# Two-layer transformer, attention stage: the refinement of the layer norms' reciprocal root moved from the vector engine to GpSimd

## What is computed

```
x = x + _L0_xattn_ref(_layernorm(x), ctx, ctx, ...)
x = x + _L0_ffn_ref(_layernorm(x), ...)
x = x + _L1_xattn_ref(_layernorm(x), ctx, ctx, mask_SxS2, mask_BxS2, ...)
x = x + _L1_ffn_ref(_layernorm(x), ...)

def _layernorm(x, eps=1e-05):
    m = jnp.mean(x, axis=-1, keepdims=True)
    v = jnp.var(x, axis=-1, keepdims=True)
    return (x - m) / jnp.sqrt(v + eps)
```

## Time and profile before

| | us |
|---|---|
| median of 3 runs | 2528.04 (2525.23 to 2528.23) |
| the profiled execution | 2527.97 |
| its span, first to last instruction | 2526.4 |
| mean granted TensorE clock | 0.953 of full speed |
| busy: PE, DVE, ACT, POOL | 2272.7, 1462.2, 861.7, 464.8 |

### The profile page before, as it was taken

How to read it: one execution, slowest core, us unless ns; L and a number is a source line. 1 busy time by engine, 2 the same in 40 slices (tenths; PEclk the granted TensorE clock), 3 DMA queues, 4 the chain that set the end, 5 groups by cost and what they waited for, 6 DMA issues and landing times. The chain is left out here.

```text
span 2526.4 us, 39469 instructions
## 1 busy us (share of the span) xinstructions
PE 2272.7 (90%) x14663; PEld 1960.2 (78%) x14663; DVE 1462.2 (58%) x3129; ACT 861.7 (34%) x1210; POOL 464.8 (18%) x413
## 2 busy tenths in 40 slices
PE   5888888565899976999999599999999999999999
PEld 3677777543788874877877588888888888888888
DVE  5777777475554526767776485545454545454444
ACT  1454544202444422444444342222222222222222
POOL 3122222200666542222221220000000000000000
PEclk8999999775899997999999799999999999999999
DMA  2021211200444330111211310000000000000000
GB/s 71 26 75 50 75 50 59 73 4 23 108 97 94 65 45 23 68 58 56 69 50 43 127 32 26 25 26 26 26 26 26 26 26 26 26 25 26 24 9 11
DMA packets 117497, 114.85 MB, mean 45 GB/s; under 512 B 15440, under 2 KB 114320, under 8 KB 117392
## 3 DMA queue, kind: packets, MB, share of 16 engines
q1 hardware_dynamic: 105104, 96.29, 12.0%
q0 software_dynamic: 12288, 17.05, 4.1%
HBM read 62.72 MB, written 50.59 MB: 45 GB/s over the span
## 5 line engine op out<-in xcount | busy, mean ns | idle before, releaser
L1802 DVE TENSOR_TENSOR zmix_hid<-zmix_act_gate,psum 128x1024 f32<-128x1024 f32 x128 | 156.3, 1221 | 389.8 <-issue 359.3
L143 PE MATMUL psum<-zmix_wd_hi,zmix_hid_hi 128*128 128x256 f32 x1024 | 289.6, 283 | 1.9 <-DVE zmix_acc L1793 1.7
L145 PE MATMUL psum<-zmix_wd_hi,zmix_hid_lo 128*128 128x256 f32 x1024 | 290.1, 283 | 0.0
L144 PE MATMUL psum<-zmix_wd_lo,zmix_hid_hi 128*128 128x256 f32 x1024 | 290.0, 283 | 0.0
L1746 ACT ACTIVATE zmix_act_gate<-psum 128x1024 f32<-128x1024 f32 x128 | 131.8, 1029 | 403.2 <-PE psum L145 403.2
L1754 ACT ACTIVATE zmix_hid_hi<-zmix_hid 128x1024 fp32r<-128x1024 f32 x128 | 135.5, 1059 | 383.8 <-PE psum L145 285.7
L593 PEld LDWEIGHTS psum<-att_v_cur,att_probs 128*128 128x128 f32 x2048 | 247.4, 193 | 9.5 <-ACT att_probs L693 3.6
L593 PE MATMUL psum<-att_v_cur,att_probs 128*128 128x96 f32 x2048 | 247.2, 275 | 2.7 <-ACT att_probs L693 2.7
L1807 DVE TENSOR_TENSOR zmix_hid_lo<-zmix_hid,zmix_hid_hi 128x1024 fp32r<-128x1024 f32 x128 | 158.7, 1240 | 135.1 <-ACT zmix_hid_hi L1754 134.2
L143 PE MATMUL psum<-zmix_xT_hi,zmix_wg_hi 128*128 128x512 f32 x512 | 203.3, 397 | 12.0 <-DVE zmix_xT_lo L1782 12.0
L1793 DVE SCALAR_TENSOR_TENSOR zmix_acc<-psum,zmix_weight,zmix_acc 128x256 f32<-128x256 f32 x512 | 211.8, 476 | 1.6 <-PE psum L145 1.6
(11 more groups left out here) (285 smaller groups left out, 4754.3 us busy)
## 6 DMA issues: line engine op xcount, KB each, us to landing
x<-att_x_new SPq DMA_DIRECT2D x32, 512.0 KB, 2.9
att_x_in<-in_x SPq DMA_DIRECT2D x16, 512.0 KB, 3.8
rows<-att_normed_new SPq DMA_DIRECT2D x16, 512.0 KB, 3.0
att_x_in<-x SPq DMA_DIRECT2D x16, 512.0 KB, 3.9
normed<-att_normed_new SPq DMA_DIRECT2D x16, 512.0 KB, 2.9
zmix_xn<-normed SPq DMA_DIRECT2D x16, 512.0 KB, 4.7
zmix_acc<-x SPq DMA_DIRECT2D x16, 512.0 KB, 4.4
out_x<-zmix_acc SPq DMA_DIRECT2D x16, 512.0 KB, 3.2
```

The lines of the kernel that those rows point to most:

```text
L143: pe.matmul(out, st_hi, mv_hi, start=first, stop=False)
L144: pe.matmul(out, st_hi, mv_lo, start=False, stop=False)
L145: return pe.matmul(out, st_lo, mv_hi, start=False, stop=last)
L1802: dve.tensor_tensor(hid[:, :, :], act_gate[:, :, :], psum[:, 2:4, :], ALU.mult).then_inc(up_out, 1)
```

## The change

After the first guess DVE makes one more small product, halved = -0.5 * (var + eps), and is done with the norm: it goes on with queries_lo and then the tiles. POOL, after its input_side(b + 1), waits for that and does three rounds of four tensor_tensor operations (y*y, times halved, plus a tile of 1.5, times y), then two for the shift (mean * rstd, and a tile of zeros minus that): 14 operations, each waiting for the one before by a new semaphore, refining. The last raises shifted, for which ACT waits as before. The norm at the very start of each attention block stays on DVE. Two memsets at the start fill the tiles of constants.

```
-def ln_steps(n):
-    return n * 2 * TT + 3 + 3 * NEWTON
+def ln_steps(n, refined=False):
+    return n * 2 * TT + (3 + 3 * NEWTON if refined else 4)
...
-    for k in range(NEWTON):
-        if k == 1 and between:
-            between()
...
+    if halved is not None:
+        dve.tensor_scalar(halved[:, cols], var, -0.5, None, ALU.mult).then_inc(sem, 1)
+        n += 1
+    if halved is None:
+        dve.wait_ge(sem, start + n)
+        refine(dve, var, guess, y, sem, start + n)
+        n += 3 * NEWTON
...
+            pool.memset(steps[:, 0, :], 1.5)
+            pool.memset(steps[:, 1, :], 0.0).then_inc(cleared, 1)
...
+            REFINE = 4 * NEWTON + 1
+
+            def norms(b):
+                ahead, new = there(b + 2), there(b - 1)
+                cols = slice(0 if ahead else TT, 2 * TT if new else TT)
+                pool.wait_ge(ln, ln_start(b) + ln_steps(ahead + new))
...
+                guess, y = tmp[:, 1, cols], rstd[:, cols]
+                n = b * REFINE
+                for k in range(NEWTON):
+                    if k:
+                        pool.wait_ge(refining, n + 4 * k)
+                    pool.tensor_tensor(guess, y, y, ALU.mult).then_inc(refining, 1)
+                    pool.wait_ge(refining, n + 4 * k + 1)
+                    pool.tensor_tensor(guess, guess, halved[:, cols], ALU.mult).then_inc(refining, 1)
+                    pool.wait_ge(refining, n + 4 * k + 2)
+                    pool.tensor_tensor(guess, guess, steps[:, 0, cols], ALU.add).then_inc(refining, 1)
+                    pool.wait_ge(refining, n + 4 * k + 3)
+                    pool.tensor_tensor(y, y, guess, ALU.mult).then_inc(refining, 1)
+                pool.wait_ge(refining, n + 4 * NEWTON)
+                pool.tensor_tensor(guess, mv[:, cols, 0], y, ALU.mult).then_inc(refining, 1)
+                pool.wait_ge(refining, n + 4 * NEWTON + 1)
+                pool.tensor_tensor(shift[:, cols], steps[:, 1, cols], guess, ALU.subtract).then_inc(shifted, 1)
+
             def body(b, p, half):
                 if there(b + 1):
                     input_side(b + 1, 1 - p, half + p)
+                norms(b)
             input_side(0, 0, 0)
-            batches(pool, body)
+            batches(pool, body, norms)
...
                 layernorm_stats(dve, xs, parts, stats, mv, rstd, tmp, ln, ln_start(b), passed, before, halved)
-                dve.wait_ge(ln, ln_start(b) + steps)
-                cols = slice(0 if ahead else TT, 2 * TT if new else TT)
-                dve.scalar_tensor_tensor(shift[:, cols], mv[:, cols, 0], -1.0, rstd[:, cols], ALU.mult, ALU.mult).then_inc(shifted, 1)
...
                 if there(b - 1):
-                    layernorms(b, p, half, ahead_of_new, between)
+                    layernorms(b, p, half, ahead_of_new)
                 else:
                     layernorms(b, p, half)
                     ahead_of_new()
-                    between()
+                between()
```

More of the change, by code:

```diff
@@ L90, in sem, with refine, layernorm_stats @@
         return self.const["sems"].take(f"{self.phase}_{name}")
-def layernorm_stats(dve, xs, parts, stats, mv, rstd, tmp, sem, start, passed, before=(), between=None):
+def refine(dve, var, guess, y, sem, start):
+    n = 0
+    for k in range(NEWTON):
+        if k:
+            dve.wait_ge(sem, start + n)
+        dve.scalar_tensor_tensor(guess, y, -0.5, y, ALU.mult, ALU.mult).then_inc(sem, 1)
+        n += 1
+        dve.wait_ge(sem, start + n)
+        dve.tensor_tensor(guess, guess, var, ALU.mult).then_inc(sem, 1)
+        n += 1
+        dve.wait_ge(sem, start + n)
+        dve.scalar_tensor_tensor(y, guess, 1.5, y, ALU.add, ALU.mult).then_inc(sem, 1)
+        n += 1
+def layernorm_stats(dve, xs, parts, stats, mv, rstd, tmp, sem, start, passed, before=(), halved=None):
     n = 0
@@ L124, in layernorm_stats @@
     n += 1
-    for k in range(NEWTON):
-        if k == 1 and between:
-            between()
+    if halved is not None:
+        dve.tensor_scalar(halved[:, cols], var, -0.5, None, ALU.mult).then_inc(sem, 1)
+        n += 1
+    if halved is None:
         dve.wait_ge(sem, start + n)
[L130 to L138, removed]
+        refine(dve, var, guess, y, sem, start + n)
+        n += 3 * NEWTON
+    assert n == ln_steps(len(xs), halved is None)
 def three_passes(pe, out, st_hi, st_lo, mv_hi, mv_lo, first, last):
@@ L402, in attention @@
         tmp = sc.sb("ln_tmp", [P, 2, 2 * TT])
+        halved, steps = sc.sb("ln_halved", [P, 2 * TT]), sc.sb("ln_steps", [P, 2, 2 * TT])
         mask_cur = sc.sb("mask_cur", [P, 2, S], BF16) if masked else None
@@ L407, in attention @@
         ln = sc.sem("ln")
-        shifted = sc.sem("shifted")
+        refining, shifted = sc.sem("refining"), sc.sem("shifted")
         norm_in, norm_out = sc.sem("norm_in"), sc.sem("norm_out")
@@ L442, in ln_start @@
         def ln_start(b):
-            first = ln_steps(2) + ln_steps(1)
+            begun = ln_steps(2, True)
+            first = begun + ln_steps(1)
             if isinstance(b, int) and b < 1:
-                return ln_steps(2)
+                return begun
             if isinstance(b, int) and b > B - 2:
@@ L508, in input_side @@
                 pool.tensor_tensor(x_bias[:, p, :, :], x_in[:, p, :, :], bo, ALU.add).then_inc(bias_done, 1)
+            REFINE = 4 * NEWTON + 1
[3 more added lines that the diff above has]
+                pool.wait_ge(ln, ln_start(b) + ln_steps(ahead + new))
+                if isinstance(b, int) and b == 0:
+                    pool.wait_ge(cleared, 4 if masked else 3)
+                guess, y = tmp[:, 1, cols], rstd[:, cols]
+                n = b * REFINE
+                for k in range(NEWTON):
+                    if k:
+                        pool.wait_ge(refining, n + 4 * k)
[10 more added lines that the diff above has]
+                pool.tensor_tensor(shift[:, cols], steps[:, 1, cols], guess, ALU.subtract).then_inc(shifted, 1)
             def body(b, p, half):
@@ L626, in route @@
                 m.then_inc(lg_made, 1)
-            pe.wait_ge(cleared, 3 if masked else 2)
+            pe.wait_ge(cleared, 4 if masked else 3)
             def body(b, p, half):
@@ L744, in _ @@
         def _(dve):
-            dve.wait_ge(cleared, 3 if masked else 2)
+            dve.wait_ge(cleared, 4 if masked else 3)
             def mask_of(b, p):
@@ L751, in mask_of, with layernorms @@
                                   ALU.mult, ALU.add).then_inc(mask_ready, 1)
-            def layernorms(b, p, half, ahead_of_new=None, between=None):
+            def layernorms(b, p, half, ahead_of_new=None):
                 ahead, new = there(b + 2), there(b - 1)
@@ L767, in layernorms @@
                 xs, parts, before = zip(*kinds)
-                steps = ln_steps(len(xs))
-                layernorm_stats(dve, xs, parts, stats, mv, rstd, tmp, ln, ln_start(b), passed, before, between)
-                dve.wait_ge(ln, ln_start(b) + steps)
-                cols = slice(0 if ahead else TT, 2 * TT if new else TT)
-                dve.scalar_tensor_tensor(shift[:, cols], mv[:, cols, 0], -1.0, rstd[:, cols], ALU.mult, ALU.mult).then_inc(shifted, 1)
+                layernorm_stats(dve, xs, parts, stats, mv, rstd, tmp, ln, ln_start(b), passed, before, halved)
             def input_norm(b, p, tiles=range(TT), col=0):
@@ L871, in _ @@
                             [lambda: dve.wait_ge(x_loaded[0], 16), lambda: dve.wait_ge(x_loaded[1], 16)])
-            dve.wait_ge(ln, ln_steps(2))
+            dve.wait_ge(ln, ln_steps(2, True))
             input_norm(0, 0)
```

## The result

The changed kernel takes 2573.72 us (median of 4 runs, 2570.57 to 2575.21) against 2528.14 us for the kernel before in the same comparison (2525.23 to 2530.63): 1.0177 times as long, with a 95% interval of 1.0163 to 1.0192. The forecast was 2593 us in a range of 2550 to 2635. The direction is right and the time lies in the range, but 20 us of the forecast loss did not come.

A forecast was written before the change was run, and what follows sets the result against it. PE's order of work was taken to bound the kernel. Bodies of the first attention 21.4, of the second 13.2, ends 11.3 and clock 19.5 us sum to 65.4 on 2527.97: 2593 us, range 2550 to 2635.

The forecast's parts named there:

- What bounds the kernel: PE's order sets the time; its 1.01 us wait for a maximum comes directly before its wait for norm_out.
- The step on POOL: Each dependent POOL operation of the norm takes 0.34 us: 0.20 length plus 0.14 gap.
- the forecast's own formula: POOL's chain of 14 operations is 13 spacings plus one length: 13 x 0.34 + 0.20 = 4.62 us.
- rival D: Quick POOL steps, 0.25 to 0.28 us, with a few falls of the clock: near 2548 us; chance 0.10.
- The clock: First attention: TensorE's clock falls in 13 of 14 bodies after PE's 2.9 us idle, 1.5 us each, 19.5 us; second: nothing.
- Rival B: POOL's steps cost as much as forecast but TensorE's clock stays up: 2574 us; chance 0.17.
- The ends: Body 15 and close of both attentions, where the whole norm stands bare: 2.83 us each, 11.3 us.
- Contention or a POOL that is late: POOL still in its addition when the guess is ready; would need that addition 0.4 us later; no chance of its own.
- rival F: Nothing visible in the time, POOL's steps at the break-even point; chance 0.04.
- one sign named ahead: In PE's timeline, a wait of 2.5 to 3 us before the transposes, released by ACT.

The follow-up runs named there:

- late transposes: Transposes of the new normalised rows moved behind tile 3 in PE's order: in the changed kernel 2492.20 us, in the kernel before 2509.57 us.
- short filler: Changed kernel plus 10 calls (20 matmuls) of discarded work in PE's wait before the first attention's transposes: 2551.97 us, 1.0096 times the kernel before.

## Why the prediction was right or wrong

**What bounds the kernel**: right. The wait for the maximum and the wait for norm_out do lie directly behind one another in PE's order; taking away the first alone bought nothing and lengthened the second. The late transposes show it from the other side.

**The step on POOL**: this is the term that was mis-sized. The forecast took 0.34 us, from a length of 0.20, which held to the hundredth, and a gap of 0.14 taken from dependent operations of another kind. The gap is 0.08, as long as the hand-over from DVE to POOL that I had used one step further down. In the changed kernel POOL's first step stands 0.08 us behind DVE's halved too (207.34 to 207.42). By the forecast's own formula 0.28 gives a chain of 3.84 us instead of 4.62, and everything that hangs on it follows: 0.76 us a body in the first attention instead of 1.53, 0.17 in the second instead of 0.94, 2.0 at each end instead of 2.83. 14 x 0.76 + 14 x 0.17 + 4 x 2.0 = 21 us instead of 46. It was rival D's step, at its upper edge. The step alone is 25 us too much; the miss is only 20 because the measured loss has 5 us that the forecast has no term for.

The rule from the Trainium skill (GPSIMD Engine Reference, Engine selection), that elementwise work with two inputs takes GpSimd about twice as long, does not agree with the trace at this size: POOL's dependent step is 0.28 us where DVE's is 0.21, 1.3 times. That the change loses even so comes as much from the number of steps, 14 where there were 10, as from their length.

**The clock**: right in mechanism and place. I had 19.5 us for the first attention and nothing for the second; the table has 18.8 and none, and the short filler took back 20. That the size came out is partly luck: the forecast was 13 falls of 1.5 us each behind a wait of 2.9 us; there were ten among the 13 distances behind a wait of 2.26, eight of 1.6 us and two twice as long. The distances of 27.8 us are 1.6 above those at full speed, as the 1.63 us of the two rows in body 15. This term turned out nearly as large as all the others together. With the right step and without it the sum would be 2549 us, near rival D's 2548; D had the step right and the clock wrong, with only a few falls. Rival B's 2574 is the measured time, but by luck: B had the step too dear by 25 us and the clock at nothing where it cost 19, and the other 5 us belong to neither. The granted clock of 0.50 and the short filler rule B out.

**The ends**: right in kind, 2.0 us each in place of 2.83 by the same step. In body 15 of the first attention the distance grew by 2.9, more than the shift's lateness. Its slow stretch was there before the change too (a granted clock of 0.50); why the rest of that body is longer stays open.

**Contention or a POOL that is late** (the note behind rival F): POOL was free 0.6 us ahead, DVE's operations beside the chain kept their lengths, and the wait followed the number of steps.

**What stays open**: 5 us of the 45.6 lie outside the attentions' periods. Ten profiles show the stretch between the attentions to vary by some 10 us in kernels that don't differ there, but no run was made for it. What makes the clock fall in one body and not in the next, behind the same wait, is open too. And one sign named ahead was met only in part: the wait before the transposes was to be 2.5 to 3 us and was 2.26, which was enough for the clock.

## What to carry to other kernels

Moving small dependent work to an idle engine shortens the busy engine's list and lengthens the latency of the result; before doing it, look which of the two the bounding engine waits for next, and if it waits for both one behind the other, move the use of the result (here one line of PE's order, which turned a loss of 46 us into a gain of 36) before moving the work. Of the 36 some 19 come with that line alone and 17 with the work on POOL. Price a chain of dependent steps by length plus hand-over, and give the hand-over a range where no row has the same kind of operation: here 0.14 and 0.08 us both stood in the trace, and the choice between them was worth 25 us. And a wait of TensorE can cost more than its own length: with waits of 1.12 and 1.51 us in a body (two rounds) the clock never fell in the loop, with 2.26 and 1.52 it did in ten of 13 distances, which cost 18.8 us beside the 9.9 of the lateness.
